# Placing the next stage's layer norms earlier among the output blocks of an attention layer

## Chip, cores and metric

The kernel runs on the 8 cores of one Trainium2 chip. The time is that of the slowest core in device microseconds. Each core works on its own 4 of the 32 sequences; there is no communication between cores.

## What is computed

One pre-norm transformer layer on x of 32 x 2048 x 1024 in f32: masked attention with 16 heads of 64, then a small feed-forward layer, each with a residual addition.

```python
x = x + attn(layernorm(x), attn_w, attn_b, out_w, out_b)
x = x + ffn(layernorm(x), Win, bin_, W1, b1, W2, b2, Wout, bout)

# attn: qkv = x @ attn_w.T + attn_b; scores = k.q / sqrt(64), masked to k <= q
#       probs = softmax over k; out = (probs.T @ v) @ out_w.T + out_b
# ffn:  s = x @ Win + bin_                 (1024 -> 64)
#       h = relu(s[..., None] * W1 + b1)   (64 -> 64 x 16)
#       g = sum(h * W2) + b2               (64)
#       out = g @ Wout + bout              (64 -> 1024)
```

## The kernel before

A core runs 16 stages: 4 sequences by 4 groups of queries. A group has 512 positions in 4 tiles of 128, numbered 0 to 3. Stages are counted from 0 here, as the loop does with `idx`. For each stage the kernel computes attention of the group against all keys up to it. Between that and the next attention lies the stretch that the change touches: the output side of this stage and the input side of the next.

Each engine's instructions are written out by hand into one list per engine, in the order in which the Python code calls `s.op` and `s.dma`; an engine runs its list in that order. Semaphore waits are added only for dependencies. So the order of calls in the main loop is the order of work on each engine.

The parts of that stretch, with the names used in the text:

- A0 to A3, `epilogueA(..., i, ...)`: output projection of tile i. 18 matmuls (L451, L457) write a 128x1024 PSUM tile, P1 for even i and P2 for odd i. VectorE adds the residual into the tile's x buffer (L462), then runs the second layer norm (`emit_ln`, L219 to L246; there without the L224 reduction, because L462 gives the sum). A2 may start only when B0 has given P1 back, and A3 when B1 has given P2 back.
- B0 to B3, `epilogueB(..., i, ...)`: the feed-forward layer of tile i. Eight transposes on TensorE (L483) go through two PSUM slots; their results are copied to SBUF by ScalarE (L490, even ones) and VectorE (L494, odd ones) in turns. Small matmuls with a copy or a relu between them follow (L506 to L541), then the last matmuls (L546, L550), the residual addition on VectorE (L554, called the output addition in the text) and the output transfer, issued by POOL.
- `LN(i)`, that is `phaseA_ln`: the load of tile i of the next stage (issued by SyncE) and its first layer norm on VectorE (L219, L224 to L234, L243, L246), with two small ScalarE operations in the middle (L237, L240).
- `TR(i, half)`, that is `phaseA_tr`: TensorE transposes of that normalised tile (L270) with ScalarE copies (L276). After the last one `phaseA_qkv` computes q, k and v of the next stage (L291, L315).

The x tiles live in six buffers: `slot(i)` is (4 idx + i) mod 6, and `nslot(i)` is the same for the next stage. So `LN(0)` and `LN(1)` fill buffers that the stage before has left, `LN(2)` fills the buffer of this stage's tile 0 and `LN(3)` that of tile 1. A load waits for the output transfer of the tile that its buffer held:

```python
tk = s.dma("sp", f"ch_x{slot}", s_x[slot][:, :], ...,
           deps=[st_["out_dma"].get(slot)] + list(extra_deps))
```

SyncE has nothing else to do between stages, so it stands at such a wait ahead of time. The last stage has no next one; `LN`, `TR` and `phaseA_qkv` do nothing there. The order in the main loop is at L585 to L605.

Of the kernel before, what the change touches and what calls it, by code (L numbers as in the profile page):

```python
# [95 lines left out]
def build_program(nseq=NSEQ):  # L96
# [20 lines left out]
    with ExitStack() as st:  # L117
# [133 lines left out]
        def phaseA_ln(sq, g, i, slot, extra_deps=()):  # L251
            tile = g * GT + i
            tk = s.dma("sp", f"ch_x{slot}", s_x[slot][:, :],
                       x_h[sq, tile * 128:(tile + 1) * 128, :],
                       deps=[st_["out_dma"].get(slot)] + list(extra_deps))
            xs = i % 2
            xln = s_xln[xs]
            txl = emit_ln(s_x[slot], xln, 8 * i, tk, st_["xln_read"][xs])
            st_["x_read"][slot] = txl
            st_["txl"][i] = txl  # L260

        def phaseA_tr(i, half=None):
            xs = i % 2
            xln = s_xln[xs]
            txl = st_["txl"][i]
            rng = range(8) if half is None else (range(4) if half == 0 else range(4, 8))
            for c in rng:
                vs = c % 4
                tr_ap = P0[:, vs * 512:vs * 512 + 128]
                ttr = s.op("pe", lambda E, a=xln, cc=c, v=tr_ap: E.matmul(  # L270
                    v, a[:, cc * 128:(cc + 1) * 128], s_id[:, :],
                    start=True, stop=True),
                    deps=[txl, st_["trA"][vs], st_["last_exp"][0], st_["last_exp"][1],
                          st_["P0_war"].get(("qk", vs)), st_["P0_war"].get(("v", vs))])
                st_["xln_read"][xs] = ttr
                st_["trA"][vs] = s.op("act", lambda E, cc=c, ii=i, v=tr_ap: E.copy(  # L276
                    s_xlnT[:, cc * QB + ii * 128: cc * QB + (ii + 1) * 128], v),
                    deps=[ttr, st_["xlnT_read"]])
# [162 lines left out]
        def epilogueA(sq, g, i, slot, comb_written):  # L441
            PO = P1 if i % 2 == 0 else P2
            po_free = st_["P1_freed"] if i % 2 == 0 else st_["P2_freed"]
            t_op = None
            for r in range(2):
                for c in range(8):
                    dep0 = [comb_written[4 * (c // 2) + 2 * (c % 2) + 1]]
                    if c == 0:
                        dep0.append(comb_written[12 + 2 * i + r] if i < 2
                                    else po_free)  # L450
                    t_op = s.op("pe", lambda E, cc=c, rr=r, ii=i, P=PO: E.matmul(  # L451
                        P[:, rr * 512:(rr + 1) * 512],
                        s_comb[:, cc * QB + ii * 128: cc * QB + (ii + 1) * 128],
                        s_ow[:, cc * 1024 + rr * 512: cc * 1024 + (rr + 1) * 512],
                        start=(cc == 0), stop=False), deps=dep0)
                    st_["comb_read"] = t_op
                t_op = s.op("pe", lambda E, rr=r, P=PO: E.matmul(  # L457
                    P[:, rr * 512:(rr + 1) * 512], s_onesb[0:1, 0:128],
                    s_brows[0:1, rr * 512:(rr + 1) * 512],
                    start=False, stop=True), deps=[])  # L460
            cS = 32 + 8 * i
            t_xp = s.op("dve", lambda E, P=PO, xi=s_x[slot], c=cS: E.scalar_tensor_tensor(  # L462
                xi[:, :], P[:, :], 1.0, xi[:, :], ALU.mult, ALU.add,
                accum_out=s_stats[:, c:c + 1]),
                deps=[t_op, st_["x_read"].get(slot)])
            xs = 2 + i % 2
            xln = s_xln[xs]
            txl = emit_ln(s_x[slot], xln, 32 + 8 * i, t_xp, st_["xln_read"][xs],
                          sum_tok=t_xp)
            ectx[i] = (t_xp, txl)  # L470
# [100 lines left out]
        for idx, (sq, g) in enumerate(stages):  # L571
            comb = attention(sq, g)
            nxt = stages[idx + 1] if idx + 1 < len(stages) else None
            slot = lambda i: (idx * GT + i) % 6
            nslot = lambda i: ((idx + 1) * GT + i) % 6

            def LN(i):
                if nxt is not None:
                    phaseA_ln(nxt[0], nxt[1], i, nslot(i))

            def TR(i, half=None):
                if nxt is not None:
                    phaseA_tr(i, half)

            LN(0)  # L585
            epilogueA(sq, g, 0, slot(0), comb)
            TR(0, 0)
            epilogueA(sq, g, 1, slot(1), comb)
            TR(0, 1)
            epilogueB(sq, g, 0, slot(0))  # L590
            LN(1)
            epilogueA(sq, g, 2, slot(2), comb)
            TR(1, 0)
            epilogueB(sq, g, 1, slot(1))
            TR(1, 1)
            LN(2)
            epilogueA(sq, g, 3, slot(3), comb)
            epilogueB(sq, g, 2, slot(2))
            TR(2, 0)
            LN(3)  # L600
            epilogueB(sq, g, 3, slot(3))
            TR(2, 1)
            TR(3)
            if nxt is not None:
                phaseA_qkv(*nxt)  # L605
# [78 lines left out]
```

How the kernel before makes its waits and increments, by code:

```python
            def run(engine):  # L80
                for emit, waits, inc_sem, inc in oplist:
                    for (sname, val) in waits:
                        engine.wait_ge(sems[sname], val)
                    ins = emit(engine)
                    if ins is not None and inc_sem is not None:
                        ins.then_inc(sems[inc_sem], inc)
```

## Time and profile before

| | us |
|---|---|
| median of 2 runs | 4300.9 |
| lowest, highest | 4290.2, 4311.7 |
| the profiled execution | 4329.5 |
| its span on the slowest core (core 5) | 4327.6 |
| spans of the 8 cores in it | 4265.3 to 4327.6 |

| engine | busy us | share of the span |
|---|---|---|
| TensorE, matmuls | 2830.9 | 65% |
| ScalarE | 1802.0 | 42% |
| VectorE | 1109.8 | 26% |
| GpSimd | 100.3 | 2% |

The times of the trace are from one profiled execution, counted from the start of the slowest core's span. An average busy share says little about a stretch in which the engines hand work to each other. A timeline row gives start, duration, engine, line, operation, tiles and count; the brackets at its end hold the idle time of the engine just before it and what ended that. A row without brackets followed its predecessor with almost no idle time. The span counts from the first to the last instruction.

### The profile page before, as it was taken

The numbers are of one execution on the slowest core, as the hardware profiler recorded it, in microseconds if no ns is written. First come the engines' busy times: TensorE is split into PE (matmuls) and PEld (weight loads), VectorE is DVE, ScalarE is ACT, GpSimd is POOL, SyncE is SP. The second block draws the span as 40 slices with busy tenths as digits, with TensorE's granted clock in tenths as the row PEclk, the third lists the DMA queues.
The fourth block names the chain that finished last, engine by engine and source line by source line (L and its number), as shares of the span: only waits on it lengthen the run. The fifth ranks groups of instructions, "written<-read, shape, count | busy, mean of one in ns | idle before, by whom it ended". The sixth has DMA issues, their size and how long they took to land.

```text
span 4327.6 us, 40105 instructions; the slowest of 8 cores (4265.3 to 4327.6 us)
## 1 busy us (share of the span) xinstructions
PE 2830.9 (65%) x12384; PEld 1087.9 (25%) x12384; DVE 1109.8 (26%) x2486; ACT 1802.0 (42%) x2945; POOL 100.3 (2%) x196
## 2 busy tenths in 40 slices
PE   0657576676747567677674757668766575765875
PEld 0222232222313222232231312223222232322322
DVE  3241312302333141320323223131132313214012
ACT  0425346175241616427433351733733244272471
POOL 0000000000000000000000000000000000000000
PEclk9768687688767768767776777867777687786775
DMA  6010000100101010000000001000000000000000
GB/s 198 15 39 15 30 25 15 39 10 11 39 20 39 19 41 10 20 30 10 20 33 27 30 20 39 13 28 20 15 25 30 30 25 25 30 15 34 6 10 25
DMA packets 36934, 122.00 MB, mean 28 GB/s; under 512 B 7610, under 2 KB 7738, under 8 KB 36732
## 3 DMA queue, kind: packets, MB, share of 16 engines
q0 software_dynamic: 19456, 67.12, 4.4%
q1 hardware_dynamic: 17020, 51.80, 3.8%
q8 instruction: 110, 1.80, 0.2%
q14 instruction: 92, 0.75, 0.1%
q10 hardware_dynamic: 256, 0.52, 0.0%
HBM read 85.34 MB, written 34.08 MB: 28 GB/s over the span
## 4 chain that ended last, share of the span: by engine, by line
PE 49%; ACT 17%; DVE 12%; issue 11%; DMA 10%; ACTq 1%; DVEq 0%; POOLq 0%; SPq 0%
PE P L315 11%; PE P L391 10%; ACT s_probs L363 7%; PE P L291 6%; PE P L451 5%; DMA s_zz<-zscr 5%; PE P L354 5%; DMA zscr<-s_zz 3%; ACT s_zz L409 3%; ACT s_zz L406 3%; DVE s_xln L219 3%; DVE s_probs L494 2%; DVE s_x L462 2%; PE P L546 2%; PE P L550 2%
## 5 line engine op out<-in xcount | busy, mean ns | idle before, releaser
L363 ACT ACTIVATE s_probs<-P 128x1024 bf16<-128x1024 f32 (+3 forms) x1280 | 1063.4, 895 | 393.2 <-PE P L358 338.1
L391 PE MATMUL P<-s_probs,s_vaug 128*65 128x512 bf16 (+3 forms) x2560 | 730.6, 402 | 198.8 <-DVE s_comb L423 108.5
L354 PE MATMUL P<-s_q,s_k 64*128 64x512 bf16 (+3 forms) x1280 | 469.6, 395 | 406.1 <-ACT s_probs L363 381.4
L371 DVE TENSOR_TENSOR s_probs<-s_probs,s_tril 128x256 bf16<-128x256 bf16 x512 | 145.6, 291 | 1407.6 <-ACT s_probs L363 1404.7
L358 PE MATMUL P<-s_q,s_k 64*128 64x512 bf16 (+3 forms) x1280 | 479.1, 403 | 0.0
L315 PE MATMUL P<-s_xlnT,s_wqk 128*128 128x512 bf16 x2048 | 462.8, 390 | 0.0
L391 PEld LDWEIGHTS P<-s_probs,s_vaug 128*65 128x65 bf16 x2560 | 248.9, 120 | 568.7 <-issue 465.3
L451 PE MATMUL P<-s_ow,s_comb 128*128 128x512 bf16 x1024 | 334.1, 485 | 39.6 <-DVE s_x L554 39.6
L237 ACT ACTIVATE s_stats<-s_stats 128x1 f32<-128x1 f32 x128 | 37.7, 295 | 755.5 <-DVE s_stats L234 755.5
L483 PE MATMUL P<-s_id,s_xln 128*128 128x128 bf16 x512 | 107.1, 258 | 370.0 <-ACT s_probs L490 276.1
L423 DVE TENSOR_TENSOR s_comb<-P,s_zz 64x512 bf16<-64x512 f32 x256 | 174.9, 683 | 670.5 <-DMA s_zz<-zscr 666.5
L354 PEld LDWEIGHTS P<-s_q,s_k 64*128 64x128 bf16 x1280 | 110.4, 95 | 800.2 <-issue 793.8
L324 ACT ACTIVATE s_q<-P,s_bqk 128x512 bf16<-128x512 f32 x128 | 88.1, 688 | 468.8 <-PE P L315 468.8
L291 PE MATMUL P<-s_wv,s_xlnT 128*128 128x512 bf16 x1024 | 275.6, 418 | 8.4 <-ACT s_xlnT L276 8.4
L315 PEld LDWEIGHTS P<-s_xlnT,s_wqk 128*128 128x128 bf16 x2048 | 203.3, 100 | 255.1 <-issue 61.9
L276 ACT CAST s_xlnT<-P 128x128 bf16<-128x128 f32 x512 | 98.8, 275 | 181.7 <-PE P L270 180.9
L451 PEld LDWEIGHTS P<-s_ow,s_comb 128*128 128x128 bf16 x1024 | 109.7, 116 | 219.1 <-issue 172.1
L406 ACT ACTIVATE s_zz<-P 1x1024 f32<-1x1024 f32 x128 | 130.1, 1016 | 76.7 <-PE P L391 36.1
L219 DVE SCALAR_TENSOR_TENSOR s_xln<-s_x 128x1024 bf16<-128x1024 f32 x128 | 156.3, 1221 | 11.3 <-DMA s_x<-x 4.1
L483 PEld LDWEIGHTS P<-s_id,s_xln 128*128 128x128 bf16 x512 | 50.1, 105 | 424.4 <-issue 419.0
L300 DVE CAST s_vaug<-P 128x512 bf16<-128x512 f32 x128 | 88.8, 694 | 258.6 <-PE P L295 254.7
L324 ACT ACTIVATE s_k<-P,s_bqk 128x512 bf16<-128x512 f32 x128 | 88.0, 688 | 142.0 <-PE P L315 142.0
(60 smaller groups left out, 2020.2 us busy)
## 6 DMA issues: line engine op xcount, KB each, us to landing
s_x<-x SPq DMA_DIRECT2D x64, 512.0 KB, 4.0
s_zz<-zscr POOLq DMA_DIRECT2D x128, 256.0 KB, 3.5
out<-s_x POOLq DMA_DIRECT2D x64, 512.0 KB, 2.9
s_x<-wqk_t SPq DMA_DIRECT2D x16, 512.0 KB, 6.6
s_x<-wv_t SPq DMA_DIRECT2D x8, 512.0 KB, 5.6
s_x<-ow_t SPq DMA_DIRECT2D x8, 512.0 KB, 5.6
zscr<-s_zz ACTq DMA_DIRECT2D x128, 4.0 KB
s_x<-bias_rows SPq DMA_DIRECT2D x1, 260.0 KB
```

Source lines behind the costliest of these rows:

```text
L219: tsq = s.op("dve", lambda E: E.scalar_tensor_tensor(dst_xln[:, :], src[:, :], 1.0, src[:, :], ALU.mult, ALU.mult, accum_out=s_stats[:, cQ ...
L291: s.op("pe", lambda E, cc=c, ii=i, rr=r, p=pacc: E.matmul(p, s_xlnT[:, cc * QB + ii * 128: cc * QB + (ii + 1) * 128], s_wv[:, cc * 1024 + ...
L315: tmm = s.op("pe", lambda E, f=fc, cc=c, p=pacc: E.matmul(p, s_wqk[:, cc * 2048 + f * 128: cc * 2048 + (f + 1) * 128], s_xlnT[:, cc * QB:( ...
L324: tev = s.op("act", lambda E, d=dst, f=fc, p=pacc: E.add(d, p, s_bqk[:, f:f + 1]), deps=[tmm])
L354: s.op("pe", lambda E, c=hp, k=kt, c0=col0, S=SC: E.matmul(S[:, c0:512], s_k[0:64, c * T + k * 128: c * T + (k + 1) * 128], s_q[0:64, c * ...
L358: t_s1 = s.op("pe", lambda E, c=hp, k=kt, c0=col0, S=SC: E.matmul(S[:, 512 + c0:1024], s_k[64:128, c * T + k * 128: c * T + (k + 1) * 128] ...
L363: texp = s.op("act", lambda E, S=SC, pb=prb, c0=col0: E.activation(pb[:, :].rearrange("p (h c) -> p h c", h=2, c=512)[:, :, c0:512], S.rea ...
L391: P=pv_banks[bank]: E.matmul(P[:, c0:512], s_vaug[:, ti * NH * 65 + hh2 * 65: ti * NH * 65 + hh2 * 65 + 65], pb[:, hi2 * 512 + c0: hi2 * 5 ...
L406: tln = s.op("act", lambda E, P=Ppv, zr=zrow: E.activation(zr, P[64:65, 0:1024], AF.Ln), deps=[t_lp, st_["zr_read"][pi], st_["zz_read"][pi]])
L423: tcm = s.op("dve", lambda E, P=pvX, c=hp, hh2=hh, z=zb: E.tensor_tensor(s_comb[(hh2 % 2) * 64:(hh2 % 2) * 64 + 64, c * QB:(c + 1) * QB], ...
L451: t_op = s.op("pe", lambda E, cc=c, rr=r, ii=i, P=PO: E.matmul(P[:, rr * 512:(rr + 1) * 512], s_comb[:, cc * QB + ii * 128: cc * QB + (ii ...
L483: ttr = s.op("pe", lambda E, a=xln, cc=c, v=tr_ap: E.matmul(v, a[:, cc * 128:(cc + 1) * 128], s_id[:, :], start=True, stop=True), deps=[tx ...
```

## The change

The calls to `LN(1)`, `LN(2)` and `LN(3)` get other places in the order of the main loop. Nothing else is edited.

```diff
             epilogueA(sq, g, 1, slot(1), comb)
+            LN(1)
             TR(0, 1)
             epilogueB(sq, g, 0, slot(0))
-            LN(1)
             epilogueA(sq, g, 2, slot(2), comb)
+            LN(2)
             TR(1, 0)
             epilogueB(sq, g, 1, slot(1))
             TR(1, 1)
-            LN(2)
+            LN(3)
             epilogueA(sq, g, 3, slot(3), comb)
             epilogueB(sq, g, 2, slot(2))
             TR(2, 0)
-            LN(3)
             epilogueB(sq, g, 3, slot(3))
```

As seen by VectorE and ScalarE the order before is LN0 A0 A1 B0 LN1 A2 B1 LN2 A3 B2 LN3 B3. Afterwards it is LN0 A0 A1 LN1 B0 A2 LN2 B1 LN3 A3 B2 B3. On ScalarE the copies of `TR(0, 1)` and `TR(1, 0)` come behind the `LN` instead of ahead of it. The order on TensorE, POOL and SyncE stays as it is.

## Rows read from the trace of the kernel before

**Rows 1.** The page's chain that ended last, shares of the span by engine
```profile
PE 49%; ACT 17%; DVE 12%; issue 11%; DMA 10%; ACTq 1%; DVEq 0%; POOLq 0%; SPq 0%
```
**Rows 2.** VectorE's timeline, stage 1, end of A1 and start of B0
```profile
486.86 0.81 DVE L246 TENSOR_SCALAR s_xln<-s_x,s_stats 128x1024 bf16<-128x1024 f32 x1
487.59 0.28 DVE L494 CAST s_probs<-P 128x128 bf16<-128x128 f32 x1
```
**Rows 3.** VectorE's timeline, stage 1, B1's first copy, directly behind A2
```profile
510.61 0.28 DVE L494 CAST s_probs<-P 128x128 bf16<-128x128 f32 x1
```
**Rows 4.** VectorE's timeline, stage 1: end of B0, LN(1), start of A2's addition
```profile
498.53 1.23 DVE L554 TENSOR_TENSOR s_x<-P,s_x 128x1024 f32<-128x1024 f32 x1 [2.44 <-PE P L550]
499.67 1.22 DVE L219 SCALAR_TENSOR_TENSOR s_xln<-s_x 128x1024 bf16<-128x1024 f32 x1
...
503.86 0.81 DVE L246 TENSOR_SCALAR s_xln<-s_x,s_stats 128x1024 bf16<-128x1024 f32 x1
505.66 1.22 DVE L462 SCALAR_TENSOR_TENSOR s_x<-P,s_x 128x1024 f32<-128x1024 f32 x1 [0.98 <-PE P L457]
```
**Rows 5.** VectorE's timeline, stage 1: end of B1, LN(2), start of A3's addition
```profile
521.55 1.22 DVE L554 TENSOR_TENSOR s_x<-P,s_x 128x1024 f32<-128x1024 f32 x1 [2.44 <-PE P L550]
522.70 1.22 DVE L219 SCALAR_TENSOR_TENSOR s_xln<-s_x 128x1024 bf16<-128x1024 f32 x1
...
529.07 1.23 DVE L462 SCALAR_TENSOR_TENSOR s_x<-P,s_x 128x1024 f32<-128x1024 f32 x1 [1.08 <-PE P L457]
```
**Rows 6.** VectorE's timeline, stage 3, the same place: B1's end and A3's addition
```profile
1103.97 1.23 DVE L554 TENSOR_TENSOR s_x<-P,s_x 128x1024 f32<-128x1024 f32 x1 [2.44 <-PE P L550]
...
1112.06 1.23 DVE L462 SCALAR_TENSOR_TENSOR s_x<-P,s_x 128x1024 f32<-128x1024 f32 x1 [1.75 <-PE P L457]
```
**Rows 7.** VectorE's timeline, stage 1: end of B2, LN(3), start of B3
```profile
544.96 1.23 DVE L554 TENSOR_TENSOR s_x<-P,s_x 128x1024 f32<-128x1024 f32 x1 [2.44 <-PE P L550]
546.10 1.22 DVE L219 SCALAR_TENSOR_TENSOR s_xln<-s_x 128x1024 bf16<-128x1024 f32 x1
...
551.39 0.28 DVE L494 CAST s_probs<-P 128x128 bf16<-128x128 f32 x1
```
**Rows 8.** VectorE's timeline, last stage (no LN): end of B2, start of B3
```profile
4305.96 1.23 DVE L554 TENSOR_TENSOR s_x<-P,s_x 128x1024 f32<-128x1024 f32 x1 [2.44 <-PE P L550]
4307.10 0.28 DVE L494 CAST s_probs<-P 128x128 bf16<-128x128 f32 x1
```
**Rows 9.** VectorE's timeline, stage 3: end of B2, start of B3
```profile
1127.95 1.22 DVE L554 TENSOR_TENSOR s_x<-P,s_x 128x1024 f32<-128x1024 f32 x1 [2.44 <-PE P L550]
...
1134.02 0.28 DVE L494 CAST s_probs<-P 128x128 bf16<-128x128 f32 x1
```
**Rows 10.** Timelines of SyncE and POOL, stage 1: loads of x, B1's output transfer
```profile
503.31 0.33 SPq L64 DMA_DIRECT2D s_x<-x  x1
...
526.31 0.33 SPq L64 DMA_DIRECT2D s_x<-x  x1
...
523.34 0.54 POOL L64 DMA_DIRECT2D out<-s_x  x1 [22.48 <-DVE s_x L554]
```
**Rows 11.** Kernel's first loads, VectorE's start behind them; all loads into s_x
```profile
77.47 0.80 SPq L64 DMA_DIRECT2D s_x<-x  x2
...
81.49 1.23 DVE L219 SCALAR_TENSOR_TENSOR s_xln<-s_x 128x1024 bf16<-128x1024 f32 x1 [4.10 <-DMA s_x<-x]
...
DMA to landing us min/median/max: 1.7/3.7/10.4
```
**Rows 12.** Busy time by stretch, B0 in stage 1; the clock stands before the DMA share
```profile
488.00:493.00 5.00, 2.78 (x17) 1.68 (x17) 1.22 (x4) 0.75 (x4) 0.00 (x0) 0.50 0.00 0
```
**Rows 13.** TensorE's timeline, stage 1, A2's second eight matmuls
```profile
503.33 1.90 PE L451 MATMUL P<-s_ow,s_comb 128*128 128x512 bf16 x8
```
**Rows 14.** TensorE's timeline, last stage, A2's second eight matmuls
```profile
4262.26 2.95 PE L451 MATMUL P<-s_ow,s_comb 128*128 128x512 bf16 x8
```
**Rows 15.** The page's DMA issues: queue, count, KB each, median us to landing
```profile
s_x<-x SPq DMA_DIRECT2D x64, 512.0 KB, 4.0
```

## The prediction

> **What bounds the kernel now.** I read the page's chain of waits first: no engine fills the span, and 11% of it is issue and hand-offs [rows 1]. So what matters is which wait ends last where the edit lies. That is the stretch between two attention stages. It occurs 16 times; the last one has no next stage, and no `LN` or `TR` in it. For this stretch I read the timelines of VectorE, TensorE and the queues in stage 1, then stage 3 and the last stage as controls. The reader is to see three things in them.
>
> First, an A block ends on VectorE with its layer norm, and the B block behind it needs both VectorE and ScalarE for the copies between its transposes (L494, L490). The last operation of A1's layer norm starts at 486.86 and B0's first VectorE copy at 487.59 [rows 2]: no idle time between them. The same holds for A2 and B1: the copy at 510.61 has no idle time ahead of it [rows 3]. Here VectorE sets the pace, and whatever is put between A1 and B0, or between A2 and B1, is paid in full.
>
> Second, after a B block the order is reversed. B0's output addition starts at 498.53. It releases the PSUM tile for A2's 18 matmuls, and A2's own addition (L462) starts at 505.66 with 0.98 us of idle time ahead of it, ended by the matmuls [rows 4]. In that time `LN(1)` ran on VectorE, from 499.67 to 504.67. Here it costs nothing; TensorE sets the pace. `LN(2)` lies the same way between B1 and A3, from 522.70, and A3's addition at 529.07 comes 7.52 us after B1's output addition at 521.55 [rows 5]. In stage 3 the same distance is 8.09 us (1103.97 to 1112.06), with 1.75 us of idle time [rows 6]. So the two present places are covered.
>
> Third, `LN(3)` lies between B2 and B3, where no A block covers it. B2's output addition starts at 544.96, `LN(3)` at 546.10, and B3's first copy waits until 551.39 [rows 7]. In the last stage, without `LN(3)`, that copy follows the addition by 1.14 us (4305.96 to 4307.10) [rows 8]. In stage 3 it follows at 6.07 us (1127.95 to 1134.02) [rows 9]. `LN(3)` is thus 6.07 - 1.14 = 4.9 us of the path in stage 3 and 6.43 - 1.14 = 5.3 in stage 1, where it has an extra gap inside. I take 5.0.
>
> **The change part by part.** It adds and removes no instruction; three groups of VectorE and ScalarE work get another place in their engines' orders. One `LN` takes 5.0 us of VectorE: from 499.67 to the end of its last operation, 503.86 + 0.81 [rows 4]. That includes the hand-over to two small ScalarE operations and back. The transposes (`TR`) stay in place and find their layer norms done earlier, so nothing is saved or lost on them.
>
> `LN(1)` from behind B0 to ahead of it. Its input was loaded a stage earlier. VectorE reaches B0's first copy 5.0 us later, and ScalarE is held too: its first copy for B0 stands behind `LN(1)`'s two operations, which wait for VectorE. B0's third transpose waits for that copy, and B0's whole chain, its output addition, the release of P1 and A2 follow 5.0 us later. At its old place nothing is gained, because the A2 matmuls covered it. **+5.0.**
>
> `LN(2)` from behind B1 to ahead of it. Its buffer is the one that B0's output leaves. The load goes out at 503.31 [rows 10] and needs 4.0 us [rows 11], so it is there at 507.3; VectorE comes to it at 510.6 [rows 3]. Both times are counted from B0's output addition and shift together, so the load stays hidden by 3.3 us. The B1 chain is later by a whole `LN`. **+5.0.** Its old place gives nothing.
>
> `LN(3)` from behind B2 to just behind B1. Two effects. Ahead of B3 it is gone: **-5.0.** At the new place its load is late. It goes into the buffer that B1's output transfer leaves; that transfer is issued at 523.34, and the load on SyncE goes out at 526.31, at once when the transfer has landed [rows 10]. SyncE already issues it at the first possible moment, and the edit can't make it earlier. The first load of the kernel, issued at 77.47, lets VectorE start at 81.49, 4.0 us later [rows 11]. So `LN(3)` can start at 526.31 + 4.0 = 530.3 and ends at 535.3, while A3's addition, now queued behind it, was at 529.07 [rows 5]: +6.3 in stage 1. From B1's output addition this is (526.31 - 521.55) + 4.0 + 5.0 = 13.8 us in any stage. Against stage 3's 8.09 that makes +5.7. I take **+6.1**, between the two. Behind the waiting instruction on VectorE stand A3's addition and its layer norm, and behind these B2's copies; TensorE finishes the A3 matmuls meanwhile and then waits for B2's copies. ScalarE holds B2's copies for the same reason. No transfer is held up on POOL, as B1's output was issued before.
>
> The Trainium skill speaks against this part: "DMA: Bandwidth & Descriptors", section "Rules for kernel authors", says to issue a transfer early and to wait for it late. The edit leaves the issue where it is and moves the wait ahead. By that rule `LN(3)` costs something at its new place, as in the sum; how much, only the rows say.
>
> Sum for a stage: 5.0 + 5.0 + 6.1 - 5.0 = 11.1 us. 15 stages have a next one: 15 x 11.1 = 166 us. The profiled span of 4327.6 becomes 4494. The profiled execution took 4329.5 us, 28.6 above the median of 4300.9. I put the sum on the median, 4300.9 + 166 = **4467 us**.
>
> What I can't read off: the granted clock. TensorE idles about 5 us longer ahead of B0 and B1. In B0, at 488 to 493, the granted clock is already 0.50 [rows 12], that is 1.2 GHz, so B itself can't get slower by this. A2's matmuls come next, and their second eight took 1.90 us in stage 1 and 2.95 in the last stage [rows 13, 14]. The longer time answers to 1.2 GHz for most of them. If that became the rule for A2, it would cost 2.95 - 1.90 = 1.05 us a stage, 16 us in all; A3's are covered by the wait for `LN(3)`. Nothing in the rows speaks for a gain, but I can't exclude one and bound it by the same 16 us. I take nothing and keep both ends.
> By the Trainium skill ("TensorE: Matmul & The Clock Gate", section "What's actually happening") the clock falls to half after idling and rises again only after activity. The trace agrees, with 0.50 in B0; by that page the sum could only grow, towards rival (c).
>
> **The rivals.**
> (a) The first two moves are free, because B0 and B1 are held by something other than VectorE, say by the order of TensorE. Then the sum is 6.1 - 5.0 = 1.1 us a stage, 16 us in all: 4317 us, not slower within 2%. If A3 also had cover, it would be 5.0 x 15 = 75 us faster, 4226, still within 2%. It decides only if at least 5.4 us of the 10.0 are covered. For it speaks that B0's first two transposes are done early. Against it: the copies start with no idle time behind A's layer norm [rows 2, 3], and without slack there is nothing to cover.
> (b) The wait for the load is longer than 4.0 us. The transfers into and out of the x buffers landed after 1.7 to 10.4 us, with a median of 3.7 [rows 11]. At 10.4 each stage loses 6.4 more, 96 us: 4563. Against it: the long ones stand in the setup, where dozens of loads run together; between the stages one load runs alone, with a median of 4.0 for this group [rows 15].
> (c) The clock, as above: 4467 + 16 = 4483.
> (d) The edit does nothing, since waits and not places set the order. VectorE takes its instructions in the order written (`LN(3)` sits exactly between B2 and B3 although its input had long landed), so I give this nothing of its own; it is part of (a).
>
> **How the numbers follow.** The forecast has 0.84, (c) 0.07, (b) 0.03, (a) 0.06. The predicted time is that of the first. Its own bounds: `LN(3)` at 5.7 or 6.3 instead of 6.1 is -6 or +3 us; 4.9 or 5.3 for its old place is +2 or -5 us; the clock is -16 or +16. That gives 4440 to 4488. The median before comes from two runs, 4290.2 and 4311.7, so 10 us may be added on either side: the range is 4430 to 4498 and takes in (c). Beyond 2% slower begins at 4387, and about 2% is what a measurement of this kernel can tell from no change. Slower has 0.84 + 0.07 + 0.03 = 0.94; (a) within 2% has 0.05, and 0.01 remains for faster.
>
> **What would show it in the changed profile.** VectorE waits before `LN(3)` for the load in all 15 stages, for 526.31 + 4.0 - 522.70 = 7.6 us each, 114 us in all; before, the first load of the kernel has such a wait, of 4.10 us [rows 11]. B0's output addition comes 5.0 us later after its stage's start, B1's follows B0's 5.0 us later than the present 23.0, B2's follows B1's at 6.1 more, and B3's follows B2's by 5.0 less. The idle time of TensorE before the B transposes, waiting for ScalarE's copies, grows by about 15 x (5 + 5 + 6 - 5). If B0's copies start with VectorE idle ahead of them, (a) was right. If the wait before `LN(3)` is well over 8 us, it is (b). If A2's second eight matmuls take near 2.95 us in most stages, it is (c). A die-wide change of the granted clock in the attention stages would make the prediction wrong in a way that nothing here bounds.

## The result

| | us |
|---|---|
| before, median of 10 runs | 4293.0 |
| after, median of 11 runs | 4464.6 |
| ratio | 1.042, 95% interval 1.037 to 1.046 |
| spans of the 8 cores in the profiled execution after | 4444.4 to 4458.0 |

By the ratio the change makes the kernel 4.2% slower; the two medians differ by 172 us, which is 4.0%. The forecast was 4467 us, with a range of 4430 to 4498.

The slowest cores of the two profiled executions don't make a fair pair: core 5 of the kernel before had a mean granted clock of 0.746, while cores 0 to 3 of the same execution had 0.763 to 0.766. For averages over the 15 stages with a next stage I take core 3 of both, with spans of 4280.7 and 4457.2 us. They are worked out from the rows of VectorE's timeline.

Stage 1 of the kernel after, VectorE's timeline on core 7: the end of A1, then `LN(1)`, then B0's first copy. It answers to [rows 2].

```profile
506.98 0.81 DVE L246 TENSOR_SCALAR s_xln<-s_x,s_stats 128x1024 bf16<-128x1024 f32 x1
507.71 1.22 DVE L219 SCALAR_TENSOR_TENSOR s_xln<-s_x 128x1024 bf16<-128x1024 f32 x1
...
511.90 0.81 DVE L246 TENSOR_SCALAR s_xln<-s_x,s_stats 128x1024 bf16<-128x1024 f32 x1
512.63 0.28 DVE L494 CAST s_probs<-P 128x128 bf16<-128x128 f32 x1
```

Before, the copy stood 0.73 us behind the start of A1's last operation. Now it is 512.63 - 506.98 = 5.65 us, 4.9 later. TensorE shows the same wait. What its third transpose waits for is ScalarE's copy, which stands behind `LN(1)` too, and the fourth waits for VectorE's copy. TensorE's timeline, same stage, first before and then after:

```profile
487.46 0.26 PE L483 MATMUL P<-s_id,s_xln 128*128 128x128 bf16 x1 [4.30 <-ACT s_probs L490]
```

```profile
512.50 0.26 PE L483 MATMUL P<-s_id,s_xln 128*128 128x128 bf16 x1 [9.23 <-ACT s_probs L490]
513.06 0.47 PE L483 MATMUL P<-s_id,s_xln 128*128 128x128 bf16 x2 [0.30 <-DVE s_probs L494]
```

The idle time ahead of the third transpose grew by 4.93 us. ScalarE's copy frees TensorE only some 0.5 us before VectorE's does, because ScalarE's two operations of the layer norm wait for VectorE's statistics. So the delay comes through both engines, and no run here holds back only one of them.

At the old place of `LN(1)` nothing is won. VectorE now idles there for 7.10 us, until the matmuls of A2 are done; this answers to [rows 4]:

```profile
523.57 1.23 DVE L554 TENSOR_TENSOR s_x<-P,s_x 128x1024 f32<-128x1024 f32 x1 [2.44 <-PE P L550]
531.90 1.23 DVE L462 SCALAR_TENSOR_TENSOR s_x<-P,s_x 128x1024 f32<-128x1024 f32 x1 [7.10 <-PE P L457]
```

Behind B1, where [rows 5] stood, VectorE waits 7.78 us for the load of `LN(3)`, and A3's addition follows only then:

```profile
552.71 1.23 DVE L554 TENSOR_TENSOR s_x<-P,s_x 128x1024 f32<-128x1024 f32 x1 [2.44 <-PE P L550]
561.71 1.22 DVE L219 SCALAR_TENSOR_TENSOR s_xln<-s_x 128x1024 bf16<-128x1024 f32 x1 [7.78 <-DMA s_x<-x]
...
566.64 1.22 DVE L462 SCALAR_TENSOR_TENSOR s_x<-P,s_x 128x1024 f32<-128x1024 f32 x1
```

SyncE and POOL, same place: B1's output transfer goes out at 554.50 and the load at 557.48, which is 4.77 us after B1's output addition. In [rows 10] it was 526.31 - 521.55 = 4.76. The load is issued exactly as before; only its reader has moved ahead of it.

```profile
554.50 0.54 POOL L64 DMA_DIRECT2D out<-s_x  x1 [28.59 <-DVE s_x L554]
```

```profile
557.48 0.33 SPq L64 DMA_DIRECT2D s_x<-x  x1
```

Ahead of B3 the copy now follows the addition at once, as it did in the last stage before [rows 8]:

```profile
582.89 1.23 DVE L554 TENSOR_TENSOR s_x<-P,s_x 128x1024 f32<-128x1024 f32 x1 [2.45 <-PE P L550]
584.03 0.28 DVE L494 CAST s_probs<-P 128x128 bf16<-128x128 f32 x1
```

The table of waits of the kernel after (who waited for whom, us in total, times, longest):

```profile
PE P L483 <- ACT s_probs L490: 471.4, 96, 11.8
PE P L483 <- DVE s_probs L494: 62.6, 145, 1.0
DVE s_x L462 <- PE P L457: 125.6, 28, 7.1
DVE s_xln L219 <- DMA s_x<-x: 124.4, 16, 8.8
```

In the same table of the kernel before, these four were:

```profile
PE P L483 <- ACT s_probs L490: 276.1, 66, 5.0
PE P L483 <- DVE s_probs L494: 91.1, 187, 1.4
DVE s_x L462 <- PE P L457: 73.9, 37, 7.6
DVE s_xln L219 <- DMA s_x<-x: 4.1, 1, 4.1
```

The single case in the last line is the kernel's first load [rows 11]. After the change there are 16 cases, this one and one for each of the 15 `LN(3)`, so `LN(2)` never waits for its load.

Averages over 15 stages, core 3, in us:

| distance | before | after | difference |
|---|---|---|---|
| A1's addition to B0's first copy | 5.01 | 9.95 | +4.94 |
| A2's addition to B1's first copy | 4.95 | 9.89 | +4.94 |
| B1's output addition to A3's addition | 7.90 | 14.15 | +6.25 |
| B2's output addition to B3's first copy | 6.13 | 1.14 | -4.99 |
| B0's output addition to A2's addition | 7.84 | 8.08 | +0.24 |
| attention's end to A1's addition | 10.15 | 10.35 | +0.20 |
| sum | | | +11.58 |

15 x 11.58 = 174 us, against 176.5 between the two spans of core 3 and 172 between the medians. Core 3 is a little above its neighbours in one row: from B1's output addition to A3's addition cores 0 to 3 have +6.01, +6.16, +5.84 and +6.25. In the mean of the four cores a stage grows by 11.4 us, 171 in all, and their spans grow by 173.

### The profile page after: what moved, and what is told of

Same layout as the page of the kernel before. It is cut to its first block, busy times and chain, and to the rows that moved or that the text cites. A ratio compares the mean times of both kernels' runs of the same rounds, so it can differ in the third digit from the quotient of the medians.

```text
span 4458.0 us, 40105 instructions; the slowest of 8 cores (4444.4 to 4458.0 us)
## 1 busy us (share of the span) xinstructions
PE 2782.7 (62%) x12384; PEld 1078.4 (24%) x12384; DVE 1110.6 (25%) x2486; ACT 1801.8 (40%) x2945; POOL 100.3 (2%) x196
## 4 chain that ended last, share of the span: by engine, by line
PE 45%; ACT 18%; DVE 13%; DMA 12%; issue 11%; ACTq 1%; DVEq 1%; SPq 0%; POOLq 0%
PE P L315 10%; PE P L391 9%; ACT s_probs L363 7%; PE P L291 6%; DMA s_zz<-zscr 5%; PE P L354 5%; PE P L451 4%; DMA zscr<-s_zz 3%; DVE s_xln L219 3%; ACT s_zz L409 3%; ACT s_zz L406 3%; DVE s_x L462 2%; PE P L546 2%; PE P L550 2%; PE P L506 1%
## 5 line engine op out<-in xcount | busy, mean ns | idle before, releaser
L391 PE MATMUL P<-s_probs,s_vaug 128*65 128x512 bf16 (+3 forms) x2560 | 706.5, 391 | 191.9 <-DVE s_comb L423 105.6
L354 PE MATMUL P<-s_q,s_k 64*128 64x512 bf16 (+3 forms) x1280 | 463.2, 386 | 417.5 <-ACT s_probs L363 389.2
L358 PE MATMUL P<-s_q,s_k 64*128 64x512 bf16 (+3 forms) x1280 | 472.7, 393 | 0.0
L483 PE MATMUL P<-s_id,s_xln 128*128 128x128 bf16 x512 | 112.4, 259 | 539.5 <-ACT s_probs L490 471.4
L315 PE MATMUL P<-s_xlnT,s_wqk 128*128 128x512 bf16 x2048 | 444.8, 379 | 0.0
L219 DVE SCALAR_TENSOR_TENSOR s_xln<-s_x 128x1024 bf16<-128x1024 f32 x128 | 156.6, 1223 | 131.5 <-DMA s_x<-x 124.4
L270 PE MATMUL P<-s_id,s_xln 128*128 128x128 bf16 x512 | 76.8, 264 | 110.7 <-DVE s_xln L246 106.8
```

The lines of the kernel that those rows point to most:

```text
L219: tsq = s.op("dve", lambda E: E.scalar_tensor_tensor(dst_xln[:, :], src[:, :], 1.0, src[:, :], ALU.mult, ALU.mult, accum_out=s_stats[:, cQ ...
L315: tmm = s.op("pe", lambda E, f=fc, cc=c, p=pacc: E.matmul(p, s_wqk[:, cc * 2048 + f * 128: cc * 2048 + (f + 1) * 128], s_xlnT[:, cc * QB:( ...
L354: s.op("pe", lambda E, c=hp, k=kt, c0=col0, S=SC: E.matmul(S[:, c0:512], s_k[0:64, c * T + k * 128: c * T + (k + 1) * 128], s_q[0:64, c * ...
L358: t_s1 = s.op("pe", lambda E, c=hp, k=kt, c0=col0, S=SC: E.matmul(S[:, 512 + c0:1024], s_k[64:128, c * T + k * 128: c * T + (k + 1) * 128] ...
L391: P=pv_banks[bank]: E.matmul(P[:, c0:512], s_vaug[:, ti * NH * 65 + hh2 * 65: ti * NH * 65 + hh2 * 65 + 65], pb[:, hi2 * 512 + c0: hi2 * 5 ...
L483: ttr = s.op("pe", lambda E, a=xln, cc=c, v=tr_ap: E.matmul(v, a[:, cc * 128:(cc + 1) * 128], s_id[:, :], start=True, stop=True), deps=[tx ...
```

## Experiments

**One move at a time.** Three kernels, each with only one of the three calls moved.

```diff
+            LN(1)
             TR(0, 1)
             epilogueB(sq, g, 0, slot(0))
-            LN(1)
```

> Of the three moves only that of LN(1), from behind B0 to ahead of it. Theory (VectorE paces the start of B0; behind B0 the layer norm was covered by A2's matmuls): +5.1 us in each of 15 stages, 77 us, ratio 1.018; the first VectorE copy of B0 starts 5.0 us later in its stage, and no other distance in the stretch changes. Rival (the start of B0 has slack, and the loss of the changed kernel sits at LN(3) alone): within 10 us of the kernel before.

Measured: 1.016 (1.013 to 1.020). From A1's addition to B0's first copy it takes 10.00 us on average (core 3), 5.0 more than before; B1's and A3's distances stay at 4.95 and 7.93.

```diff
+            LN(2)
             TR(1, 0)
             epilogueB(sq, g, 1, slot(1))
             TR(1, 1)
-            LN(2)
```

> Only LN(2) moved, from behind B1 to between A2 and B1. Theory: its load has landed when VectorE comes to it, so it costs what LN(1) costs, +5.2 us a stage, 78 us, ratio 1.018, and VectorE doesn't wait for a load. Rival (the load isn't there in time): more than 5.2 us a stage, with a wait of VectorE for the load of x.

Measured: 1.017 (1.015 to 1.019). The distance in B1 is 9.88 instead of 4.95. Its VectorE timeline in stage 1 shows `LN(2)` starting without idle time; the load was there:

```profile
527.21 0.81 DVE L246 TENSOR_SCALAR s_xln<-s_x,s_stats 128x1024 bf16<-128x1024 f32 x1
527.94 1.22 DVE L219 SCALAR_TENSOR_TENSOR s_xln<-s_x 128x1024 bf16<-128x1024 f32 x1
...
532.87 0.28 DVE L494 CAST s_probs<-P 128x128 bf16<-128x128 f32 x1
```

```diff
             TR(1, 1)
             LN(2)
+            LN(3)
             epilogueA(sq, g, 3, slot(3), comb)
             epilogueB(sq, g, 2, slot(2))
             TR(2, 0)
-            LN(3)
```

> Only LN(3) moved, from ahead of B3 to behind LN(2), ahead of A3. Theory: LN(3) still can't start before its load has landed, 8.7 us after the start of B1's output addition, so A3's addition comes 13.8 us after it as in the changed kernel (+6.1), and B3 starts 5.0 us earlier: +1.1 us a stage, 17 us, ratio 1.004; VectorE waits only about 2.6 us for the load, as LN(2) fills the rest. Rival (the changed kernel's loss at A3 is the length of the wait of VectorE, 7.6 us, and not the moment of the load): A3 is later by only LN(3)'s 5.0 us less the slack of 1.6, +3.4, and the sum is -1.6 us a stage, -24 us.

Measured: 1.006 (1.002 to 1.011). A3's addition comes 13.92 us after B1's output addition (+6.0), and B3's first copy 4.99 us earlier: +1.0 a stage. The wait of VectorE in stage 1 is 2.57 us, a third of that in the changed kernel, and A3 is as late as there:

```profile
533.70 1.23 DVE L554 TENSOR_TENSOR s_x<-P,s_x 128x1024 f32<-128x1024 f32 x1 [2.44 <-PE P L550]
534.84 1.22 DVE L219 SCALAR_TENSOR_TENSOR s_xln<-s_x 128x1024 bf16<-128x1024 f32 x1
...
542.70 1.22 DVE L219 SCALAR_TENSOR_TENSOR s_xln<-s_x 128x1024 bf16<-128x1024 f32 x1 [2.57 <-DMA s_x<-x]
...
547.64 1.22 DVE L462 SCALAR_TENSOR_TENSOR s_x<-P,s_x 128x1024 f32<-128x1024 f32 x1
```

So the length of a wait is not its cost. What counts is the moment of the load: 547.64 - 533.70 = 13.94 here, 566.64 - 552.71 = 13.93 in the changed kernel. The ratios of the three add up to 1.6 + 1.7 + 0.6 = 3.9%, against the 4.2% (3.7 to 4.6) of all three together. The difference lies within the intervals, so no run shows that the moves act on each other.

**The load's lateness taken away.** `LN(3)` normalises the tile that `LN(2)` read before, and its own load stays in place. The kernel leaves out the right input of the next stage's tile 3.

```diff
-            txl = emit_ln(s_x[slot], xln, 8 * i, tk, st_["xln_read"][xs])
-            st_["x_read"][slot] = txl
+            early = i == 3 and not extra_deps and st_["txl"].get(3)
+            src = s_x[st_["ln2_slot"]] if early else s_x[slot]
+            txl = emit_ln(src, xln, 8 * i, st_["txl"][2] if early else tk,
+                          st_["xln_read"][xs])
+            st_["x_read"][slot] = tk if early else txl
+            st_["ln2_slot"] = slot
```

> The changed kernel, but LN(3) normalises the tile that LN(2) has just used, which has landed; its own tile is still loaded at the same time for the later residual. Left out is the right input of the next stage's tile 3. Theory: the wait of about 7.6 us per stage goes, LN(3) is covered by A3's matmuls as LN(2) was, and what is left is +5.1 +5.2 -5.0 = 5.3 us a stage, 79 us, ratio 1.018 against the kernel before. Rival (the place between B1 and A3 is costly by itself): the ratio stays near 1.04.

This run gave a profile but no interval for the time, so the kernel was timed once more:

> The changed kernel with LN(3) normalising LN(2)'s landed tile (left out: the right input of the next stage's tile 3), once more, since its first timing gave no ratio. Theory, from the profile of the first run: B0 and B1 later by 4.95 us each, A3 without loss, B3 earlier by 5.0, so 4.9 + 4.9 - 0.3 - 5.0 = 4.6 us a stage plus some 0.4 for the clock, 75 us, ratio 1.017. Rival (the place between B1 and A3 is costly by itself): near 1.04.

Measured: 1.0175 (1.011 to 1.024). The wait for a load behind B1 is gone; VectorE goes on at once, and A3's addition follows 7.41 us after B1's output addition on average, against 14.15 in the changed kernel (core 3). Stage 1 in the profile of the first run:

```profile
561.73 1.23 DVE L558 TENSOR_TENSOR s_x<-P,s_x 128x1024 f32<-128x1024 f32 x1 [2.44 <-PE P L554]
562.87 1.22 DVE L219 SCALAR_TENSOR_TENSOR s_xln<-s_x 128x1024 bf16<-128x1024 f32 x1
...
570.36 1.23 DVE L466 SCALAR_TENSOR_TENSOR s_x<-P,s_x 128x1024 f32<-128x1024 f32 x1 [2.48 <-PE P L487]
```

The bracket of the last row names two early transposes of B2 (L487), which TensorE runs directly behind A3's last matmul; that matmul ends at 570.19. The place between B1 and A3 is covered for one layer norm whose input is there. The cost at this place is the load's lateness alone, worth 1.042 - 1.0175 = 2.4%, or 14.15 - 7.41 = 6.7 us a stage.

**A dose of VectorE work at both places.** `LN(1)` and `LN(2)` get a second reduction into an unused column, once in the kernel before and once in the changed one.

```diff
+                if scol in (8, 16):
+                    s.op("dve", lambda E: E.reduce_sum(
+                        s_stats[:, scol + 7:scol + 8], src[:, :], axis=AX.X), deps=[dep_src])
                 tr1 = s.op("dve", lambda E: E.reduce_sum(
```

> The kernel before with one more reduction of 1.2 us on VectorE in each LN(1) and LN(2), its result unused. Theory: behind B0 and B1 it is covered by the matmuls of A2 and A3, with 1.0 to 2.4 us of idle time ahead of the addition: 0 to 0.3 us a place, at most 9 us in all, ratio 1.00. Rival (a VectorE operation costs its duration wherever it stands): 2 x 1.2 x 15 = 36 us, ratio 1.008.

Measured: 0.999 (0.994 to 1.003). The idle time ahead of the A additions has taken the dose in. In the table of waits it fell from 73.9 us to 41.5, by 32 of the 30 x 1.13 = 34 us put in (on core 3 of both, from 72.1 to 38.4), and A2's and A3's additions follow as before (7.85 and 7.87 us):

```profile
DVE s_x L465 <- PE P L460: 41.5, 32, 6.4
```

> The changed kernel with the same additional reductions in LN(1) and LN(2), which now stand ahead of B0 and B1. Theory: paid in full, 1.2 us at each place, 36 us in all over the changed kernel, ratio 1.0418 + 0.0085 = 1.050 against the kernel before; the stretches before B0's and B1's output additions grow by 1.2 each. Rival (B0 and B1 are held by ScalarE's or TensorE's order, and not by VectorE's work): no more than 5 us over the changed kernel, 1.042.

Measured: 1.043 (1.035 to 1.050), too wide to separate 1.050 from the changed kernel's 1.042. The traces decide. In the two profiled executions, with mean granted clocks of 0.751 to 0.754 on all cores, each of the 8 cores has a longer span with the dose, by 20.8 to 45.5 us and by 31 in the mean, where the rival allowed 5. From A1's addition to B0's first copy it takes 11.10 us (core 3), from A2's to B1's 11.04, each 1.15 more than in the changed kernel. That is the distance of the two reductions in it (513.34 to 514.47), so B0 and B1 pay in full for VectorE work put ahead of them:

```profile
513.34 1.22 DVE L225 TENSOR_REDUCE s_stats<-s_x 128x1 f32<-128x1024 f32 x1
514.47 1.21 DVE L227 TENSOR_REDUCE s_stats<-s_x 128x1 f32<-128x1024 f32 x1
...
518.25 0.28 DVE L497 CAST s_probs<-P 128x128 bf16<-128x128 f32 x1
```

The whole stretch grew by less than 15 x 2.3 = 34 us, by some 23 on core 3, because A2's matmuls went a little faster in this run (7.58 us from B0's output addition to A2's addition, against 8.08).

**The other direction.** `LN(3)` behind B3.

```diff
             TR(2, 0)
-            LN(3)
             epilogueB(sq, g, 3, slot(3))
+            LN(3)
             TR(2, 1)
```

> The kernel before with LN(3) moved the other way, from ahead of B3 to behind B3, ahead of TR(3). Theory: there VectorE is idle, but TensorE's next work, the transposes of that tile and the v matmuls behind them, waits for LN(3): the v matmuls start 1.15 + 5.0 + about 2.5 us after B3's output addition instead of 2.7, +6.0, against -5.0 ahead of B3: +1.0 us a stage, 15 us, ratio 1.004. Rival (a layer norm behind a B block is covered wherever it stands): -5.0 us a stage, ratio 0.983.

No interval came out of its timing. Its two fastest executions took 4313.7 and 4317.5 us, where the kernel before had a median of 4294.5 beside them; the rival's 0.983 would be 4221. In the profile its cores span 4286.3 to 4311.8 us. On core 3 the v matmuls start 8.54 us after B3's output addition instead of 2.70, +5.8, and B3's own part is 5.0 shorter. TensorE in stage 1 waits 5.98 us for this layer norm, so there is no cover behind B3:

```profile
574.74 1.60 PE L270 MATMUL P<-s_id,s_xln 128*128 128x128 bf16 x8 [5.98 <-DVE s_xln L246]
```

**Work into the idle time of B.** If VectorE's order costs time ahead of a B block, its idle time inside one is the place to go. `emit_ln` becomes a generator with a stop between the statistics and ScalarE's part; `epilogueB` advances it behind L511 and behind L541.

```diff
+            yield
             tsr = s.op("act", lambda E: E.activation(
...
                 s_sg[0:64, 0:128], P[0:64, :], s_binb2[0:64, 0:1], None, ALU.add),
                 deps=[t_smm])
+            if fill is not None:
+                next(fill, None)
...
-            epilogueB(sq, g, 2, slot(2))
+            epilogueB(sq, g, 2, slot(2), fill=LNg(3))
             TR(2, 0)
-            LN(3)
```

> The kernel before with LN(3) cut in two and put inside B2, where VectorE idles: the statistics between L511 and L541 (3.7 us of idle time, 3.15 us of work), the rest between L541 and L554 (2.4 us of idle time, 1.1 of work). Theory: LN(3)'s 5.0 us leave the path and nothing replaces them, B3's output addition follows B2's after 12.1 us instead of 17.1: -75 us, ratio 0.983. Rival (the filling delays the small copies that B2's chain waits for): B2 gets longer by part of the 4.3 us, and the gain is below 40 us.

Measured: 0.980 (0.972 to 0.987). B3's first copy follows B2's output addition after 1.14 us, and B2 takes as long as it did, 11.0 us from its first copy to its output addition. The layer norm is free there.

The second kernel does this with all of it. `epilogueA` too becomes a generator, stopped behind its matmuls:

```diff
-            epilogueA(sq, g, 1, slot(1), comb)
+            a = A(1)
+            next(a)
             TR(0, 1)
-            epilogueB(sq, g, 0, slot(0))
+            epilogueB(sq, g, 0, slot(0), fill=a)
             LN(1)
...
-            LN(3)
-            epilogueB(sq, g, 3, slot(3))
+            epilogueB(sq, g, 3, slot(3), fill=LNg(3))
```

> All VectorE work that stands ahead of a B block and is not needed by it goes into the idle time of a B block, cut in the same two places: the addition and layer norm of A1 in B0, of A2 in B1, of A3 in B2, LN(3) in B3; LN(1) and LN(2) stay behind B0 and B1. Theory: the first copy of each B follows the last matmul of the A block ahead of it after some 0.3 us instead of 4.9, that is -4.4, -4.6 and -4.6 us, and -5.0 for LN(3): 18.6 x 15 + 13.6 in the last stage = 293 us, about 4000 us, ratio 0.932. Rival (the B blocks get longer by what is put in, or the A2 and A3 matmuls with LN(1) and LN(2) leave no room): a gain of half or less, ratio above 0.965.

Measured: 0.926 (0.917 to 0.935), with spans of 3976.4 to 3988.1 us on the cores. Stage 1, VectorE, inside B0: the copy at 473.46 (L517 here) belongs to B0, A1's addition and layer norm follow in its shadow, and the next operation of B0, at 477.50, still has 0.63 us of idle time ahead of it:

```profile
468.03 0.81 DVE L247 TENSOR_SCALAR s_xln<-s_x,s_stats 128x1024 bf16<-128x1024 f32 x1
469.37 0.29 DVE L500 CAST s_probs<-P 128x128 bf16<-128x128 f32 x1 [0.52 <-PE P L489]
...
473.46 0.34 DVE L517 TENSOR_SCALAR s_sg<-P,s_binb 64x128 bf16<-64x128 f32 x1 [1.40 <-PE P L512]
473.73 1.21 DVE L468 SCALAR_TENSOR_TENSOR s_x<-P,s_x 128x1024 f32<-128x1024 f32 x1
...
477.50 0.34 DVE L549 TENSOR_SCALAR s_sg<-P,s_binb 64x128 bf16<-64x128 f32 x1 [0.63 <-PE P L545]
477.77 0.14 DVE L244 SCALAR_TENSOR_TENSOR s_stats<-s_stats 128x1 f32<-128x1 f32 x1
...
480.29 1.22 DVE L564 TENSOR_TENSOR s_x<-P,s_x 128x1024 f32<-128x1024 f32 x1 [1.45 <-PE P L560]
```

B0 from its first copy to its output addition takes 10.97 us, the same as before. Per stage on core 3 the four parts, up to the output additions of B0 to B3, are 4.4, 4.7, 5.1 and 5.0 us shorter than in the kernel before, and the last stage's part of the span falls from 95.5 to 79.7 us. That makes 304 us, and 294 of them are seen in the span; the time ahead of the first output side is 3 us longer, and the way from B3 to the end of the next attention 0.5 us a stage. I have not looked into these 10 us.

## Why the prediction was right

- *VectorE sets the pace ahead of B0 and B1, so a layer norm there is paid in full, 5.0 each.* Right. 4.94 each; the single moves cost 1.6% and 1.7%, and the dose came out at 1.15 us for a reduction that occupies VectorE for 1.13. TensorE's idle time ahead of the B transposes, with both copying engines as the cause, grew from 367 to 534 us, by 167; 15 x 11 = 165 was forecast.
- *The old places of `LN(1)` and `LN(2)` were covered, so nothing is won.* Right. A2's addition isn't earlier (7.84 to 8.08), and a dose at those places cost nothing.
- *`LN(2)`'s load is there in time.* Right; no idle time ahead of it, and no case of it in the table of waits.
- *`LN(3)` gives back 5.0 ahead of B3.* Right, 4.99.
- *A3's addition at 13.8 us after B1's output addition, because the load can't go out earlier: +6.1.* Right: 14.15 on average, +6.25. The wait of VectorE was given as 7.6 us and 114 in all; it is 7.78 in stage 1 and 124.4 in all, with the first load of the kernel in it. The load took 561.71 - 557.48 = 4.2 us in this stage from its issue to VectorE's start, not 4.0; core 3 has 4.2 in the mean, too. And in 3 of the 15 stages the output transfer ahead of it took 3.8 to 4.0 us instead of 2.9, which puts the mean issue 0.2 us later. That makes 14.15 instead of 13.8. The difference from the forecast is only 0.15, since the distance before was 7.90 and not the 7.7 that +6.1 implies. In the mean of cores 0 to 3 the term is +6.07, so the miss is within what single cores differ by, 5.84 to 6.25.
- *The sum of 11.1 a stage, 166 us.* It is 11.58 and 174. Besides the 0.15 at A3, two terms that were left at nothing hold the rest. A2's addition comes 0.24 us later, the direction of rival (c), at less than a quarter of its 1.05. But it isn't the second eight matmuls that (c) looked at: on core 3 they take 2.24 us in the mean before and after, and none of the 15 stages after has more than 2.63. It is the part ahead of them: the first eight took 3.18 to 3.57 us before, 3.44 in the mean, and take 3.57 in every stage after, which is 0.13 of the 0.24. And A1's addition comes 0.20 later. I have not tested why; on cores 0 to 3 it is 0.12 to 0.25.
- The end result was closer than its parts, 4467 against 4464.6: the sum was put on a median of two runs that was 8 us above the one of ten, and this made up for the 8 us that the sum of the stages lacked. That is luck.
- Rival (a) falls by the two single moves and by the dose. Rival (b) falls by the table of waits, where the longest wait for a load of x is 8.8 us. Its argument was loosely put: the loads of up to 10.4 us are three of the first six x loads, which are issued one behind the other from 77.5 to 79.7 us; six loads run together there, not dozens. Rival (d) falls with (a).

The Trainium skill's rule on overlapping transfers with compute ("DMA: Bandwidth & Descriptors", section "Rules for kernel authors") says to wait for a transfer late, and the trace agrees: with the issue in place and the reader moved ahead, A3's addition came 6.25 us a stage later, and with the reader's data already there it came no later than before (7.41 us behind B1's output addition against 7.90). No run here issues the load itself earlier.

## What to carry to other kernels

In this kernel an operation has no price of its own, only one for its place. The same layer norm cost 0 us behind the output additions of B0 and B1 (the next step waited for TensorE), 5.8 behind that of B3 (TensorE waited for it), 4.9 ahead of the transposes (the next step waited for VectorE), and again 0 when cut in two inside a block of hand-overs. Before moving work earlier, look at the idle time ahead of the next operation on that engine at both places, and at when the input is really there; a load whose buffer comes free late gains nothing from a reader that asks early. Where a row has no idle time ahead of a hand-over and another shows 2 to 4 us inside one, move work from the first to the second: here that made the kernel 7.4% faster than before.

## What was not expected of the hardware

Longer idling of TensorE cost little clock. TensorE idled 9.23 us ahead of B0's third transpose instead of 4.30, and the granted clock was 0.50 at the end of it and in B0, the same as in B0 before [rows 12]. Busy time by stretch, stage 1 after, the wait and then B0:

```profile
508.00:512.00 4.00, 0.00 (x0) 0.00 (x0) 2.79 (x8) 0.96 (x6) 0.00 (x0) 0.50 0.00 0
512.00:518.00 6.00, 3.03 (x18) 1.79 (x18) 2.13 (x6) 1.25 (x7) 0.00 (x0) 0.50 0.00 0
```

A2's matmuls begin at 1.2 GHz in either kernel, and how many of their second eight still go at that level differs from stage to stage and run to run: 1.90 to 2.83 us before and 1.98 to 2.63 after, on core 3 over the 15 stages. The dose in the changed kernel got back 0.5 us of its 2.3 a stage in this way, by chance or by the shifted moment; no run here separates the two.

The load of `LN(3)` isn't equally fast on all cores. After the change VectorE starts 3.8 to 3.9 us after the load's issue on cores 0, 2, 4 and 6, in the mean of the 15 stages, and 4.1 to 4.2 us after it on cores 1, 3, 5 and 7. So A3's addition comes 13.76 to 13.78 us after B1's output addition on the first four and 14.03 to 14.15 on the others. No run here shows why.
